# Attention on one core: value products one per step in two of every three steps, in place of one or two in every third step

## The chip, the core and the metric

The kernel runs on one core of a Trainium2 chip. The metric is the device time of one execution in microseconds, the median of several executions. The engines of the core are TensorE (PE, with its weight loads shown apart as PEld), VectorE (DVE), ScalarE (ACT), GpSimd (POOL) and SyncE (SP), which issues most DMAs.

## The reference

One transformer layer over a sequence of 4096 rows of 256 features: attention with 16 heads of 16 features, a residual and a layer norm, then a feed-forward product with int8 weights, a residual and a layer norm. The attention, which is nearly all of the time, is

```python
attn = jnp.einsum('bhqd,bhkd->bhqk', query, key) / scale     # 16 heads, 4096 x 4096 each
attn = jax.nn.softmax(attn, axis=-1)
out = jnp.einsum('bhqk,bhkd->bhqd', attn, value)
out = out.transpose(0, 2, 1, 3).reshape(b, s, d_model)
return out @ Wo_w + Wo_b
```

with query and key each a sum of a plain and a rotary projection. The kernel computes the softmax without a row maximum of its own: a bound on each row's scores is a further row of the stacked query, and the row sum comes from a column of ones beside the values.

## The kernel before, in words

A first stage projects x into keys, queries and values. The attention stage then works on 32 "heads" t: 16 heads times two halves of 2048 queries. A head has 32 key tiles kt of 128 keys, and 4 query blocks j of 512 queries, so 128 blocks of 128x512 scores. The tiles in BY_VECTOR (15, 30 and 31; for t = 0 tile 15 alone) have their exponential computed by VectorE as a polynomial. All other blocks go through ScalarE in groups of two (GROUPS): 62 groups for head 0, 58 for each other head, 1860 groups in all. A group is one step s of the schedule.

For each step TensorE does, in this order (the loop at L613): it waits for ScalarE's exponential of step s (`pe.wait_ge(a.exp, s + 1)`); it computes the two score blocks of step s + 3 (`scores`, L555: K of 49 rows, fp16, one block in each half of the array's rows, side by side); if BLOCK_STEP names the step, it computes one score block for VectorE (`block`); if PROJECT_STEP names it, it projects a finished tile of the first half (`project_first`, L637; 16 such steps, in heads 17 to 22); and it computes the value products that VALUES[s] lists (`values`, L598). A value product is one key tile with all four query blocks: four fp32 matmuls of 128x32 by 128x512 on the four column quarters of the array, which the profile lists as eight records. Scores go to three pairs of PSUM banks in turn (SLOTS = 3), so the scores of step s + 3 may be written only when ScalarE is done with step s.

ScalarE does one ACTIVATE (L797) per step: exp over two banks (128x1024) into a ring of 30 blocks, 15 steps, in SBUF. It waits for the scores of its step, and, where `ring_need` says so, for the value product that frees its place in the ring.

VectorE takes its own blocks out of PSUM one by one (`block_bits`, L833). After four blocks, a cycle, it splits bits (L841, L843), and in the next cycle, behind each block's bits, it does one step of the polynomial of the cycle before (L853, L857). The last of these tells TensorE (b_exp) that the tile may be used for a value product. At a head's end it copies the head's sums out (L807) and norms them (L812 to L826). TensorE computes block n only when the bits of block n - 1 are taken out; it computes the first value product of a head only when the bits of the last block before it are out, and the first block after that only when the copy is done, for these two use the same two banks, 6 and 7, in exchange.

The order is fixed when the program is built. `value_steps` gives the 32 steps of a head's value products: `HEAD_STEP[t] + LAG + k * length // KT`, moved on to the next step with s % 3 == 0. As 32 products fall on some 20 such steps, most of these have two. `make_values` then fills the steps with tiles, each tile no earlier than the step of its last exponential, and tiles of VectorE VECTOR_LATE steps behind the block whose polynomial step finishes them. `make_block_steps` spreads the 12 blocks of a head evenly between TURN[t] + BEHIND and TURN[t + 1] - BEFORE, where TURN[t] is the step of the head's first value product, and moves a block that would fall on s % 3 == 0 on by one.

Of the kernel before, what the change touches and what calls it, by code (L numbers as in the profile page):

```python
# [32 lines left out]
SLOTS, SLOT = 3, 2  # L33
# [22 lines left out]
CYCLES = len(TILES)  # L56
PLACE = {(t, kt, j): (g * SLOT + k) % RING for g, (t, blocks) in enumerate(GROUPS) for k, (kt, j) in enumerate(blocks)}

LAG = 6
VALUE_PHASE = 0  # L60
FIRST_BLOCKS = 14
BEFORE = 4
BEHIND = 5
VECTOR_LATE = 4
URGENT = 6


def value_steps(t):

    length = HEAD_STEP[t + 1] - HEAD_STEP[t]  # L70
    steps = []
    for k in range(KT):
        s = HEAD_STEP[t] + LAG + k * length // KT
        s += (VALUE_PHASE - s) % SLOTS
        steps.append(min(s, STEPS_ALL))
    return steps


VALUE_STEPS = [value_steps(t) for t in range(NT)]
TURN = [steps[0] for steps in VALUE_STEPS] + [STEPS_ALL]  # L80


def make_block_steps():

    steps = []
    for t in range(NT):
        first = TURN[t] + BEHIND if t else 0
        last = TURN[t + 1] - BEFORE if t + 1 < NT else STEPS_ALL - 20
        n = FIRST_BLOCKS if t == 0 else len(BY_VECTOR) * QB
        n = min(n, QB * CYCLES - len(steps))  # L90
        for k in range(n):
            s = first + (last - first) * k // (n - 1)
            s += s % SLOTS == VALUE_PHASE and k < n - 1
            steps.append(s)
    return steps


BLOCK_STEP = make_block_steps()
assert BLOCK_STEP == sorted(BLOCK_STEP) and len(BLOCK_STEP) == QB * CYCLES
COPY_AFTER = {FIRST_BLOCKS - 1 + len(BY_VECTOR) * QB * t: t for t in range(NT - 1)}  # L100
# [12 lines left out]
def make_values():  # L113

    at = [[] for _ in range(STEPS_ALL + 1)]
    for t in range(NT):
# [6 lines left out]
        for s in VALUE_STEPS[t]:  # L123
            urgent = scalar and scalar[0][1] + RING // SLOT - 1 < s + URGENT
            if vector and not urgent and (vector[0][0] <= s or not scalar):
# [1597 lines left out]
```

## Time and profile before

| | before |
|---|---|
| median of 3 runs | 1998.19 us (1994.56 to 1999.97) |
| the profiled execution: its time | 1997.78 us |
| its span, first to last instruction | 1995.9 us |
| attention stage: first exponential starts, last ends | 157.26 and 1899.72 us |
| ACT busy | 1827.3 us, 92% |
| PE busy | 1806.7 us, 91% |
| DVE busy | 1578.7 us, 79% |
| mean granted TensorE clock | 0.981 of full speed |

Busy times are unions of an engine's instructions. Successive instructions of ScalarE overlap in the profile by some 0.1 us, and matmuls by more, so that an engine can be shown busy without a break and still be held up a little at each instruction. Starts of instructions tell more than busy shares.

### The profile page before, as it was taken

How to read it: one execution, taken by the hardware profiler on the slowest of the kernel's cores; microseconds unless marked ns; L12 is line 12 of the kernel's file. 1: busy time of each engine (PE TensorE's matmuls, PEld its weight loads, DVE VectorE, ACT ScalarE, POOL GpSimd, SP SyncE). 2: the span in 40 equal slices, each digit the busy share in tenths (PEclk: the TensorE clock that was granted, in tenths of full speed). 3: DMA queues.
4: the chain of work that ended last, by engine and by line, in shares of the span. 5: the costliest groups of instructions: out<-in, count | busy, mean ns of one | idle time of the engine just before them, and what ended most of it. 6: DMA issues, size and time to landing. Idle time of an engine off the chain costs nothing.

```text
span 1995.9 us, 31796 instructions
## 1 busy us (share of the span) xinstructions
PE 1806.7 (91%) x13009; PEld 490.0 (25%) x13009; DVE 1578.7 (79%) x1500; ACT 1827.3 (92%) x2026; POOL 167.3 (8%) x134
## 2 busy tenths in 40 slices
PE   8967999999999999999999999999999999999965
PEld 3431222222222222222222222222222222222234
DVE  3654887988887888888788888788988988888548
ACT  4448999999999999999999999999999999999925
POOL 5723500000000000000000000000000300000012
PEclk9998999999999999999999999999999999999977
DMA  4654111110111111111121000111111100110012
GB/s 163 215 170 163 25 25 25 25 25 18 21 22 19 21 25 25 24 25 25 25 67 25 19 18 17 22 25 25 25 25 25 25 21 21 21 21 17 1 44 85
DMA packets 165484, 81.48 MB, mean 41 GB/s; under 512 B 130205, under 2 KB 146717, under 8 KB 164857
## 3 DMA queue, kind: packets, MB, share of 16 engines
q1 hardware_dynamic: 164024, 78.11, 15.0%
q8 instruction: 103, 1.69, 0.3%
q10 hardware_dynamic: 1312, 1.32, 0.2%
q14 instruction: 45, 0.36, 0.1%
HBM read 48.83 MB, written 29.23 MB: 39 GB/s over the span
## 4 chain that ended last, share of the span: by engine, by line
ACT 66%; PE 13%; issue 10%; DVE 4%; POOL 2%; DMA 2%; SPq 1%; ACTq 0%; DVEq 0%; POOLq 0%
ACT arena L797 53%; ACT parts_or_sums L797 13%; PE PS L598 7%; PE PS L555 4%; PE PS L637 2%; PE PS L1041 1%; POOL arena L1360 1%; DVE arena L857 1%; DVE bn L725 1%; DMA arena<-arena 1%; DMA Qst<-parts_or_sums 1%; POOL arena L1359 1%; POOL arena L1362 1%; DVE arena L1651 1%; DMA arena<-head_out 0%
## 5 line engine op out<-in xcount | busy, mean ns | idle before, releaser
L797 ACT ACTIVATE arena<-PS 128x1024 f32<-128x1024 f32 x1488 | 1395.0, 1038 | 30.5 <-PE PS L555 29.1
L598 PE MATMUL PS<-arena,Vh 128*32 128x512 f32 x6704 | 1001.2, 600 | 0.8 <-DVE arena L857 0.4
L555 PE MATMUL PS<-Qst,Kst 49*128 49x512 f16 x4096 | 691.3, 384 | 126.8 <-ACT arena L797 77.1
L857 DVE SCALAR_TENSOR_TENSOR arena<-arena 128x2048 f32<-128x2048 f32 x282 | 646.5, 2292 | 0.1
L833 DVE TENSOR_SCALAR arena<-PS 128x512 int32<-128x512 f32 x376 | 259.3, 690 | 286.1 <-PE PS L555 278.1
L555 PEld LDWEIGHTS PS<-Qst,Kst 49*128 49x128 f16 x4096 | 178.5, 93 | 945.5 <-ACT arena L797 710.8
L598 PE MATMUL PS<-parts_or_sums,Vh 128*32 128x512 f32 x1488 | 366.1, 600 | 0.0
L797 ACT ACTIVATE parts_or_sums<-PS 128x1024 f32<-128x1024 f32 x372 | 360.9, 1037 | 3.8 <-PE PS L555 3.4
L598 PEld LDWEIGHTS PS<-arena,Vh 128*32 128x32 f32 x6704 | 195.0, 109 | 340.5 <-issue 331.1
L853 DVE SCALAR_TENSOR_TENSOR arena<-arena 128x2048 f32<-128x2048 f32 x94 | 216.0, 2298 | 0.0
L841 DVE TENSOR_SCALAR arena<-arena 128x2048 int32<-128x2048 int32 x94 | 115.7, 1231 | 7.3
L843 DVE TENSOR_SCALAR arena<-arena 128x2048 int32<-128x2048 int32 x94 | 115.8, 1232 | 0.0
L1380 POOL TENSOR_SCALAR nmr<-mv 128x16 f32<-128x16 f32 x1 | 0.3, 264 | 1231.6 <-DVE mv L1529 1231.6
L1041 PE MATMUL PS<-arena,w 128*128 128x512 f32 x192 | 87.8, 606 | 8.8 <-DMA bias<-biases_dram 6.7
L598 PEld LDWEIGHTS PS<-parts_or_sums,Vh 128*32 128x32 f32 x1488 | 66.0, 109 | 74.4 <-issue 74.4
L1244 ACT ACTIVATE arena<-PS,bias 128x512 f32<-128x512 f32 x56 | 38.1, 687 | 42.8 <-PE PS L1041 33.1
L1041 PEld LDWEIGHTS PS<-arena,w 128*128 128x128 f32 x192 | 37.2, 195 | 56.0 <-issue 55.0
L1464 DVE TENSOR_TENSOR arena<-arena 128x512 f32<-128x512 f32 x16 | 17.3, 1086 | 40.0 <-POOL arena L1362 40.0
L767 POOL TENSOR_TENSOR arena<-arena,rows 128x256 f32<-128x256 f32 x32 | 45.0, 1449 | 39.8 <-DMA arena<-x_dram 39.8
L771 POOL TENSOR_TENSOR arena<-arena,rows 128x256 f32<-128x256 f32 x16 | 11.1, 727 | 342.5 <-ACT arena L757 342.5
L807 DVE COPY parts_or_sums<-PS 128x512 f32<-128x512 f32 x32 | 22.0, 686 | 13.5 <-PE PS L598 13.5
L741 ACT ACTIVATE rstd<-mv,small 128x6 f32<-128x6 f32 (+3 forms) x6 | 1.8, 300 | 32.2 <-DVE mv L729 32.2
(115 smaller groups left out, 615.4 us busy)
## 6 DMA issues: line engine op xcount, KB each, us to landing
Kst<-k_halves SPq DMA_DIRECT2D x64, 128.0 KB
Qst<-q_halves SPq DMA_DIRECT2D x64, 128.0 KB
Vh<-head_values SPq DMA_DIRECT2D x30, 256.0 KB, 4.4
arena<-xT_dram SPq DMA_DIRECT2D x8, 512.0 KB, 5.1
k_halves<-parts_or_sums SPq DMA_DIRECT2D x16, 256.0 KB, 2.4
k_whole<-arena SPq DMA_DIRECT2D x8, 512.0 KB, 3.3
q_halves<-parts_or_sums SPq DMA_DIRECT2D x16, 256.0 KB, 3.2
q_whole<-arena SPq DMA_DIRECT2D x8, 512.0 KB, 4.4
```

What stands on the lines that cost most here:

```text
L555: return nc.tensor.matmul(out, Kst[par][low:low + HK + 1, at:at + 128], Qst[par][low:low + HK + 1, j * CH:(j + 1) * CH], start=True, stop= ...
L598: last = nc.tensor.matmul(bank(value_bank(t))[32 * j:32 * j + 32, :], Vh[t % 2][:, kt, :], moving, start=kt == first, stop=kt == last_kt)
L637: last = nc.tensor.matmul(out, heads_out(t // TH, c, t % TH * 128, 128), w[:, W_O + c * D:W_O + (c + 1) * D], start=c == 0 and starts, sto ...
L767: nc.gpsimd.tensor_tensor(Y[:, t, :], Y[:, t, :], bo, ALU.add).then_inc(s, 1)
L797: nc.scalar.activation(ring(at, k), bank(g % SLOTS * SLOT, k), ACT.Exp, scale=EXP_SCALE).then_inc(a.exp, 1)
L833: nc.vector.tensor_scalar(bits[:, j * CH:(j + 1) * CH].bitcast(int32), bank(block_bank(n)), LOWEST, TO_BITS, ALU.max, ALU.mult).then_inc(b ...
L841: nc.vector.tensor_scalar(mantissa.bitcast(int32), bits.bitcast(int32), 0x007FFFFF, 0x3F800000, ALU.bitwise_and, ALU.bitwise_or).then_inc( ...
L843: nc.vector.tensor_scalar(power.bitcast(int32), bits.bitcast(int32), 0x7F800000, 0x40000000, ALU.bitwise_and, ALU.bitwise_xor).then_inc(b_ ...
L853: nc.vector.scalar_tensor_tensor(out=t, in0=mantissa, scalar=POLY[3], in1=mantissa, op0=ALU.add, op1=ALU.mult).then_inc(b_poly, 1)
L857: last = nc.vector.scalar_tensor_tensor(out=t, in0=t, scalar=POLY[3 - j], in1=power if j == 3 else mantissa, op0=ALU.add, op1=ALU.mult)
L1041: last = nc.tensor.matmul(bank(out_bank), l, r, start=k == 0, stop=k == len(lhsT) - 1)
L1244: nc.scalar.activation(dst[e], bank(e), ACT.Identity, bias=bs[e], scale=scales[e]).then_inc(s_ev, 1)
```

## The change

The value products may now stand on steps with s % 3 of 0 or 1, at most one per step; blocks for VectorE on steps with s % 3 of 2 or 1; and five distances of the plan are shorter. Nothing else is changed: each engine does the same instructions on the same data.

```diff
-LAG = 6
-VALUE_PHASE = 0
+LAG = 4
+VALUE_PHASES = (0, 1)
+BLOCK_PHASES = (2, 1)
 FIRST_BLOCKS = 14
-BEFORE = 4
-BEHIND = 5
+BEFORE = 3
+BEHIND = 4
 VECTOR_LATE = 4
-URGENT = 6
+URGENT = 4
 def value_steps(t):
...
         s = HEAD_STEP[t] + LAG + k * length // KT
-        s += (VALUE_PHASE - s) % SLOTS
+        s = max(s, steps[-1] + 1 if steps else 0)
+        while s % SLOTS not in VALUE_PHASES:
+            s += 1
         steps.append(min(s, STEPS_ALL))
 def make_block_steps():
...
             s = first + (last - first) * k // (n - 1)
-            s += s % SLOTS == VALUE_PHASE and k < n - 1
+            s += s % SLOTS not in BLOCK_PHASES and k < n - 1
             steps.append(s)
```

## Rows read from the trace of the kernel before

**Rows 1.** The page's first part: busy us, share of the span, instructions.
```profile
PE 1806.7 (91%) x13009; PEld 490.0 (25%) x13009; DVE 1578.7 (79%) x1500; ACT 1827.3 (92%) x2026; POOL 167.3 (8%) x134
```
**Rows 2.** Busy time of L797 alone in stretches: us, ACT busy (xcount), clock, DMA.
```profile
157.26:300.00 142.74, 141.74 (x154) 0.96 0.19 53
...
600.00:900.00 300.00, 299.05 (x324) 1.00 0.11 23
...
1090.00:1390.00 300.00, 286.78 (x309) 1.00 0.11 22
...
1600.00:1899.72 299.72, 298.76 (x323) 1.00 0.08 17
sum 1742.46, ACT 1724.04; mean ACT 246.29
```
**Rows 3.** Timeline of ACT around 1075 us: start, us, instruction, count.
```profile
1074.84 2.87 ACT L797 ACTIVATE parts_or_sums<-PS 128x1024 f32<-128x1024 f32 x3
1077.55 11.26 ACT L797 ACTIVATE arena<-PS 128x1024 f32<-128x1024 f32 x12
1088.70 2.92 ACT L797 ACTIVATE parts_or_sums<-PS 128x1024 f32<-128x1024 f32 x3
1091.51 7.54 ACT L797 ACTIVATE arena<-PS 128x1024 f32<-128x1024 f32 x8
```
**Rows 4.** Timeline from 940.9 us, weight loads of PE that begin each piece.
```profile
941.52 0.33 PEld L555 LDWEIGHTS PS<-Qst,Kst 49*128 49x128 f16 x5 [0.84 <-ACT arena L797]
...
942.48 0.16 PEld L598 LDWEIGHTS PS<-arena,Vh 128*32 128x32 f32 x8 [0.29 <-issue]
...
944.34 0.33 PEld L555 LDWEIGHTS PS<-Qst,Kst 49*128 49x128 f16 x5 [0.84 <-ACT arena L797]
...
945.30 0.11 PEld L598 LDWEIGHTS PS<-arena,Vh 128*32 128x32 f32 x1 [0.35 <-issue]
...
946.30 0.10 PEld L555 LDWEIGHTS PS<-Qst,Kst 49*128 49x128 f16 x2 [0.84 <-ACT arena L797]
```
**Rows 5.** Timeline from 1115 us, a step with a projection and those behind it.
```profile
1115.04 0.10 PEld L555 LDWEIGHTS PS<-Qst,Kst 49*128 49x128 f16 x2 [0.84 <-ACT arena L797]
...
1115.36 0.73 PEld L637 LDWEIGHTS PS<-w,ctkv 128*128 128x128 f32 x4 [0.23 <-issue]
...
1116.42 0.10 PEld L555 LDWEIGHTS PS<-Qst,Kst 49*128 49x128 f16 x2 [0.33 <-issue]
...
1116.86 1.02 ACT L797 ACTIVATE arena<-PS 128x1024 f32<-128x1024 f32 x1 [0.36 <-PE PS L555]
...
1117.54 0.16 PEld L598 LDWEIGHTS PS<-arena,Vh 128*32 128x32 f32 x8 [0.42 <-issue]
...
1117.78 1.02 ACT L797 ACTIVATE parts_or_sums<-PS 128x1024 f32<-128x1024 f32 x1
...
1118.54 0.11 PEld L555 LDWEIGHTS PS<-Qst,Kst 49*128 49x128 f16 x4 [0.84 <-ACT arena L797]
1118.85 0.10 PEld L555 LDWEIGHTS PS<-Qst,Kst 49*128 49x128 f16 x2 [0.20 <-ACT parts_or_sums L797]
1119.03 1.94 ACT L797 ACTIVATE parts_or_sums<-PS 128x1024 f32<-128x1024 f32 x2 [0.24 <-PE PS L555]
```
**Rows 6.** Stretch 600 to 900 us: us, busy of PE, PEld, DVE, ACT, POOL.
```profile
600.00:900.00 300.00, 279.83 (x2142) 66.25 (x2136) 248.99 (x208) 299.05 (x324) 0.00 (x0) 1.00 0.11 23
```
**Rows 7.** The page's groups of VectorE's polynomial and bits: busy, mean ns | idle before.
```profile
L857 DVE SCALAR_TENSOR_TENSOR arena<-arena 128x2048 f32<-128x2048 f32 x282 | 646.5, 2292 | 0.1
L833 DVE TENSOR_SCALAR arena<-PS 128x512 int32<-128x512 f32 x376 | 259.3, 690 | 286.1 <-PE PS L555 278.1
```
**Rows 8.** Line L857, who waited for it: us, times.
```profile
  PEld PS L598: 7.8, 20
```
**Rows 9.** The chain that ended last, 1888 to 1908 us.
```profile
1888.29 1.23 DVE arena L843
1889.54 2.30 DVE arena L853
1891.87 2.30 DVE arena L857
1894.19 2.30 DVE arena L857
1896.52 2.30 DVE arena L857
1899.23 8.05 DMA arena<-head_out
1907.99 2.00 PE PS L637 x4
```

## The prediction

> **What bounds the kernel now.** I read the page's busy shares first. ACT is busy 92% and PE 91% of the span [rows 1], which doesn't tell which of them holds the other. Then I looked at the exponentials alone. The attention stage holds 1860 of them between 157.26 and 1899.72 us, 1742.5 us, and in it ACT has hardly a gap: 299.05 of 300 us [rows 2]. That looks like an engine at its limit. The starts say otherwise. Three exponentials that nothing holds up start within 1077.55 - 1074.84 = 2.71 us, 0.904 us each; a little later three take 1091.51 - 1088.70 = 2.81 us [rows 3]. At 0.904 us each the 1860 would need 1859 x 0.904 + 1.03 = 1682 us. So **60.8 us** of the stage is lost in small waits, and the 0.13 us by which instructions overlap in the profile hides most of it.
>
> Where do they come from? In rows 4 and 5 the reader can see TensorE's order, piece by piece:
> - Scores begin 0.05 us after the end of the exponential that frees their banks: an end at 1117.78 + 1.02 = 1118.80, the load at 1118.85 [rows 5].
> - Scores with something else behind them take 0.32 us (1115.04 to 1115.36) [rows 5]; scores followed by scores 0.23 us (five loads of 0.09 us within 0.33 us, so the fifth starts some 0.23 us after the first) [rows 4]. A block for VectorE is one more matmul of the same kind, 0.22 us.
> - Two value products take 944.34 - 942.48 = 1.86 us until the next scores; one takes 946.30 - 945.30 = 1.00 us [rows 4], and again 1118.54 - 1117.54 = 1.00 [rows 5]. So a product is 0.86 us, and each return from values to scores costs 0.14 us once.
> - From the start of late scores to their exponential it is 0.44 us (1116.42 to 1116.86) to 0.49 us (1118.54 to 1119.03) [rows 5].
>
> Put together, with times from the end of exponential s, s a step with two values: scores at 0.05, values at 0.37, the scores of step s + 4 at 2.23, exponential s + 4 at 2.67 to 2.72. ACT alone would start it at 4 x 0.904 - 1.03 = 2.59. It is late by 0.08 to 0.13 us. The plan of before (worked out from the functions shown) has 402 steps with two values: 402 x 0.10 = 40 us, with the slip of the next exponential somewhat more. The rest is elsewhere: from 1090 to 1390 us there are 309 exponentials where other stretches of 300 us have 324 [rows 2], 15 x 0.904 = 14 us for the 16 projections. Some 1 to 2 us are at the stage's start.
>
> **The change part by part.** I write "lag" for how long after the end of exponential s the scores of step s + 3 begin. ACT is not held up as long as the lag is at most 3 x 0.904 - 1.03 - 0.44 = 1.24 us (1.19 with 0.49).
>
> *Removed: the pairs.* Worked out from the new plan, 1022 steps have one value and none within the attention has two. After one value the next lag is 0.05 + 0.32 + 1.00 - 0.904 = 0.47 us. The 0.10 us at 402 places, about 46 us with what follows them, go.
>
> *Added: switches.* Steps with values rise from 619 to 1023, so there are 404 more returns at 0.14 us and as many more turns from scores to values at 0.32 - 0.23 = 0.09 us: 93 us more of TensorE. This lies in TensorE's slack, if it has it. Per three steps TensorE needs, before, 0.32 + 1.86 + 0.23 + 0.23 = 2.64 us with two values and 1.78 us with one. With 402 of 620 triples of the first kind and 376 x 0.22 us of blocks it averages 2.47 us of the 2.71. Afterwards a triple with two values takes 0.32 + 1.00 + 0.32 + 1.00 + 0.23 = 2.87 us, more than ACT's 2.71; the average is 2.62 us, 96.6%. So TensorE still keeps up on average, but nearly two thirds of the triples run behind and the triples with one value catch up.
>
> The Trainium skill says in "TensorEngine Tiling (Array Packing)", section Key Properties, that changing the tiling mode, and not just the tile, drains TensorE; scores (two row halves) and values (four column quarters) are two such modes. The page gives no price; the trace agrees with 1.00 us against 0.86. By the rule this change is made the wrong way round: it buys an even order with drains.
>
> How far does it fall behind? A value step adds 0.32 + 1.00 - 0.904 = 0.42 us to the lag, a step without one takes 0.67 off, a block adds 0.22. The new plan has nearly always two triples with two values, then one with one value. From a lag of 0.05 the six steps give 0.05, 0.47, 0.88, 0.21, 0.63, 1.04: below 1.24. But of the 185 such double runs 172 have one block ahead of that last point: 1.26, late by 0.02 to 0.07 us. That is 3 to 12 us; I take 8. It is a sum of nine pieces, each good to 0.02 us: 0.1 us more would be 17 us more, while 0.1 less gains only those 8. After the triple with one value the lag is 0.05 again, so nothing piles up.
>
> *The projections* keep their 16 steps and 1.06 us each (1115.36 to 1116.42) [rows 5]. Ten of them now stand on s % 3 == 2, behind two value steps: lag about 0.9 to 1.1, then + 0.23 + 1.06 + 0.09 - 0.904, and the next value steps push it on by 0.42 each: 0.8 us or so late each time, against 14/16 = 0.87 before. 13 us stay.
>
> *VectorE.* Its work per head is 248.99 us of 300 [rows 6], 45 us in a head of 58 steps (54.2 us); in a head of 53 us that is 85%. Its blocks have 51 steps in place of 49, so in time they are as far apart as before, 4.2 us, for 3.0 us of bits and polynomial and 2.5 us of split each fourth time. The polynomial that releases a value takes 0.05 + 0.23 + 0.44 + 0.69 + 2.29 = 3.7 us from the exponential ahead of its block [rows 7]; the value is asked for 4 steps later at 3.62 + 0.37 = 3.99 us. This 4-step case, 11 tiles before, is 30 tiles now. TensorE waited for these 20 times, 7.8 us [rows 8]. What is queued behind such a wait are scores, which have some 0.8 us of lag to give, so little of it reaches ACT. At a head's turn the last block stands 3 steps ahead of the value that needs its bank, 2.7 us, for 1.2 us if VectorE is free, 3.5 us if it has just begun a polynomial step. Together I take 4 us, between nothing and 10.
>
> *LAG, URGENT, ring.* In the plan a ring place is asked for at the earliest 3 steps behind its value before, 6 afterwards: no new wait. The DMAs hang on the same counts of scores and on norms that come no later. The start keeps 1 to 2 us, as the first values run at half clock or near it (0.96 on average in the first stretch) [rows 2]. At the end the chain goes from the last block, step 1840 in both plans, over VectorE's polynomial and the load of the heads to the projection [rows 9]; what the last 20 steps gain (0.7 us) is therefore not on the path, and the two values fewer behind the last exponential aren't either.
>
> *The sum.* Lost before 60.8; lost after 8 + 13 + 4 + 2 = 27, and as the errors of the lag reach further up than down I take 33. Gain 60.8 - 33 - 0.7 = 27 us. The profiled execution took 1997.8 us, 0.4 under the median of 1998.2; the forecast is **1971 us**.
>
> The Trainium skill ("Trainium Kernel Development and Optimization", Best Practices) warns against reading matmul busy time as closeness to the limit. Here PE is shown busy 279.8 of 300 us [rows 6], 93%, and 93 us more would give 98%, which sounds like less room than the 96.6% of the sum above.
>
> **Rivals.**
> 1. *All waits but the projections' go.* If each piece is 0.01 us shorter, no run of triples is late: 15 us left, gain 45, **1953 us**. For it: the lateness is 0.02 to 0.07 only. Against: the 0.49.
> 2. *The switch is dearer in this order* (the other side). If the return costs 0.18 and not 0.14 us, four returns add 0.16 us to each of 172 double runs: 27 us, the whole gain, **1998 us**. That is the point from which it decides; at 0.20 it is some 14 us slower, **2012 us**. Against it stand two returns behind single values of 1.00 us in different surroundings [rows 4, 5]; for it, that no row shows value, scores, value without a pause.
> 3. *VectorE becomes the one that is late.* If it runs 1 us behind at the 62 tiles that are wanted 4 or 5 steps after their block, TensorE stands 0.8 us each time with a lag of 0.6 already there, and ACT loses about 0.3: 19 us, **1990 us**. For it: 17% idle become 15%. Against: in the trace it waits for blocks 278 us in all [rows 7].
>
> **How the numbers follow.** The forecast has 0.58 (its own range 1961 to 1982: lost after 22 to 43), rival 1 0.14, rival 2 0.16 (half of it slower, the rest from 1985 to 2003), rival 3 0.12. What can be told from no change is 0.3%, 6 us. Faster by more: 0.58 + 0.14 + 0.07 + 0.05 = 0.84; within: 0.08; slower: 0.08. The range takes in rival 1, the upper bounds of the unknown costs and most of rival 3: 1952 to 1990.
>
> **What would show it.** In 600 to 900 us there should be 327 to 331 exponentials in place of 324, with three starting in 2.71 to 2.75 us everywhere; the stretch of the projections should still be 13 to 15 exponentials short. A single value should still take 1.00 us up to the next scores. Value steps followed by late exponentials should be those of a second triple with two values and a block. L857 should show waits of TensorE of 5 to 15 us. The forecast is wrong if the return costs more than 0.16 us, if exponentials on s % 3 == 2 are late in every triple, or if waits for VectorE exceed 20 us.

## The result and the profile after

The kernel after takes **1986.2 us** (median of 4 runs, 1983.7 to 1987.6) against 1997.7 us before (median of 4 runs too; the 1998.2 of the table above is of 3): ratio 0.994, 95% interval 0.9924 to 0.9956. That is 11.5 us less, where 27 were forecast. The forecast had the direction right and the size wrong, and 1986.2 us lies in its range of 1952 to 1990.

The page's busy shares, which answer to [rows 1]:
```profile
PE 1851.2 (93%) x13009; PEld 451.9 (23%) x13009; DVE 1582.6 (80%) x1500; ACT 1815.3 (92%) x2026; POOL 163.4 (8%) x134
```
The busy time of the exponentials alone (L800 is the old L797), which answers to [rows 2]:
```profile
600.00:900.00 300.00, 300.00 (x328) 1.00 0.12 23
...
1090.00:1390.00 300.00, 287.20 (x310) 1.00 0.10 21
...
sum 1732.20, ACT 1712.21; mean ACT 244.60
```
The quiet stretch has 328 exponentials in place of 324, within the forecast's 327 to 331, and the stretch of the projections is 18 short of that, where 13 to 15 were forecast. The stage took 1732.2 us in place of 1742.5: 10.3 us less. The profiled execution was 14.1 us faster than the one of before; the other 3.8 us lie outside the stage, behind it. There the clock came back sooner: in the 25 us behind the last exponential the granted clock was 0.86 on average, 0.73 before. Both executions begin the projections of the tail at 1.2 GHz (granted clock 0.52 from 1907 to 1920 us before). Before, four tiles took 2.07 or 2.08 us and one 1.76, after, one took 2.07 and one 1.75:
```profile
1897.42 2.07 PE L640 MATMUL PS<-w,arena 128*128 128x256 f32 x4
...
1899.96 1.75 PE L640 MATMUL PS<-w,arena 128*128 128x256 f32 x4
...
1901.95 1.13 PE L640 MATMUL PS<-w,arena 128*128 128x256 f32 x4
```
Whether this belongs to the change is not shown: the stretch behind the last exponential takes 96.2 us in the profiles of before and thin_before, 92.1 and 91.8 in those of after and thin_after (the thin kernels come below), and 93.0 to 95.2 in all others of this study. Between the medians lie 11.5 us, and the profiled stages account for 10.3 of them.

TensorE's pieces, which answer to [rows 4]. The timeline, weight loads that begin a piece:
```profile
441.19 0.10 PEld L558 LDWEIGHTS PS<-Qst,Kst 49*128 49x128 f16 x2 [0.84 <-ACT arena L800]
...
441.52 0.12 PEld L601 LDWEIGHTS PS<-arena,Vh 128*32 128x32 f32 x3 [0.23 <-issue]
...
442.51 0.33 PEld L558 LDWEIGHTS PS<-Qst,Kst 49*128 49x128 f16 x5 [0.84 <-ACT arena L800]
...
443.26 0.11 PEld L601 LDWEIGHTS PS<-parts_or_sums,Vh 128*32 128x32 f32 x2 [0.42 <-issue]
```
Scores 0.33 us, one value 442.51 - 441.52 = 0.99 us, as forecast; over the stage's 1020 single values the median from the first load to the next scores' load is 0.996 us, as it is for the 216 before. The switch costs what it did before.

So where are the missing 15 us? The first surprise is in ScalarE's own rows. The timeline of ACT in the kernel after:
```profile
656.14 3.01 ACT L800 ACTIVATE parts_or_sums<-PS 128x1024 f32<-128x1024 f32 x3
658.99 11.16 ACT L800 ACTIVATE arena<-PS 128x1024 f32<-128x1024 f32 x12
669.89 3.02 ACT L800 ACTIVATE parts_or_sums<-PS 128x1024 f32<-128x1024 f32 x3
```
Three exponentials without a wait took 2.87 us before [rows 3]; here they take 3.01 and 3.02. The same instruction lasts 1.13 us on average in place of 1.04 (the page of after has mean 1134 and 1137 ns for L800, that of before 1038 and 1037 for L797). Nothing in it was changed.

### The profile page after: what moved, and what is told of

The parts are those of the page before. It is cut to its first block, busy times and chain, and to the rows that moved or that the text cites. A ratio compares the mean times of both kernels' runs of the same rounds, so it can differ in the third digit from the quotient of the medians.

```text
span 1981.9 us, 31796 instructions
## 1 busy us (share of the span) xinstructions
PE 1851.2 (93%) x13009; PEld 451.9 (23%) x13009; DVE 1582.6 (80%) x1500; ACT 1815.3 (92%) x2026; POOL 163.4 (8%) x134
## 4 chain that ended last, share of the span: by engine, by line
ACT 69%; PE 10%; issue 9%; DVE 6%; DMA 2%; POOL 2%; SPq 1%; ACTq 0%; DVEq 0%; POOLq 0%
ACT arena L800 55%; ACT parts_or_sums L800 14%; PE PS L601 5%; PE PS L558 3%; PE PS L640 1%; DVE arena L860 1%; PE PS L1044 1%; POOL arena L1363 1%; DVE bn L728 1%; DMA Qst<-parts_or_sums 1%; DMA arena<-arena 1%; POOL arena L1362 1%; DVE arena L1654 1%; POOL arena L1365 0%; DMA arena<-head_out 0%
## 5 line engine op out<-in xcount | busy, mean ns | idle before, releaser
L800 ACT ACTIVATE arena<-PS 128x1024 f32<-128x1024 f32 x1488 | 1396.5, 1134 | 31.4 <-PE PS L558 31.0
L601 PE MATMUL PS<-arena,Vh 128*32 128x512 f32 x6704 | 1082.6, 606 | 5.5 <-DVE arena L860 3.6
L558 PE MATMUL PS<-Qst,Kst 49*128 49x512 f16 x4096 | 710.7, 384 | 61.4 <-ACT arena L800 38.2
L860 DVE SCALAR_TENSOR_TENSOR arena<-arena 128x2048 f32<-128x2048 f32 x282 | 646.4, 2292 | 0.1
L601 PE MATMUL PS<-parts_or_sums,Vh 128*32 128x512 f32 x1488 | 386.0, 604 | 0.0
L800 ACT ACTIVATE parts_or_sums<-PS 128x1024 f32<-128x1024 f32 x372 | 369.3, 1137 | 2.8 <-PE PS L558 2.8
L601 PEld LDWEIGHTS PS<-arena,Vh 128*32 128x32 f32 x6704 | 155.9, 108 | 278.6 <-issue 270.0
L601 PEld LDWEIGHTS PS<-parts_or_sums,Vh 128*32 128x32 f32 x1488 | 53.1, 108 | 59.1 <-issue 59.1
L1362 POOL TENSOR_TENSOR arena<-arena 32x512 f32<-32x512 f32 x16 | 24.4, 1527 | 40.2 <-DMA arena<-arena 40.1
```

The source lines that it names most:

```text
L558: return nc.tensor.matmul(out, Kst[par][low:low + HK + 1, at:at + 128], Qst[par][low:low + HK + 1, j * CH:(j + 1) * CH], start=True, stop= ...
L601: last = nc.tensor.matmul(bank(value_bank(t))[32 * j:32 * j + 32, :], Vh[t % 2][:, kt, :], moving, start=kt == first, stop=kt == last_kt)
L800: nc.scalar.activation(ring(at, k), bank(g % SLOTS * SLOT, k), ACT.Exp, scale=EXP_SCALE).then_inc(a.exp, 1)
L860: last = nc.vector.scalar_tensor_tensor(out=t, in0=t, scalar=POLY[3 - j], in1=power if j == 3 else mantissa, op0=ALU.add, op1=ALU.mult)
L1362: nc.gpsimd.tensor_tensor(b, b, tab[par][:, 1, :], ALU.mult).then_inc(s_rope, 1)
```

## The experiments

"Lost by ends" below is what the stage lost, that is, how much longer it took than its 1860 exponentials alone would, if an exponential takes 0.9167 us from end to end. For the whole stage it is the stage less 1.03 less 1859 x 0.9167 = 1704.1 us; for parts it is summed over the end times of the exponentials' records. The first experiment shows where 0.9167 comes from.

**half_after and half_before: how fast is ScalarE alone?** Half the columns of every value product, in both kernels. As the sums are then incomplete, a second edit, not shown here, holds at zero the flag that starts the kernel's exact second attention. The edit in values:

```diff
-                    moving = poly[c % 2][:, j * CH:(j + 1) * CH] if vector else ring(at)
-                    last = nc.tensor.matmul(bank(value_bank(t))[32 * j:32 * j + 32, :],
+                    moving = (poly[c % 2][:, j * CH:(j + 1) * CH] if vector else ring(at))[:, 0:CH // 2]
+                    last = nc.tensor.matmul(bank(value_bank(t))[32 * j:32 * j + 32, 0:CH // 2],
```

> The kernel after, with each value product cut to half its columns (256 of 512), and the flag that starts the exact second attention held at zero; so the attention sums are incomplete. TensorE has some 0.7 us less to do per three steps and nothing in the stage waits for it, the projections' steps excepted. Theory A (ScalarE's own rate is what the ends of its exponentials show, 0.917 us each, and the 0.904 us between starts is only a start running ahead of the end before): 1860 exponentials take 1706 us and a few more, 1707 to 1716 us from first start to last end, 327 in a quiet stretch of 300 us. Theory B (0.904 us is the rate, as the prediction took it): 1682 to 1692 us, 332 in 300 us.

> The kernel before with the same two edits (half the columns of each value product, flag held at zero). Both theories: the pair of values takes 1.0 us less, so no exponential is late behind it; the order of the value products makes no difference and the stage is within 4 us of the same edit in the kernel after. Theory A: 1707 to 1718 us. Theory B: 1682 to 1694 us.

Measured: 2010.2 and 2018.3 us, one execution each, stages of 1758.2 and 1763.0 us. Both theories missed the time, because less work made TensorE slower: its granted clock fell again and again (last section). Of the 53.0 us that half_after lost by ends 49.1 fall on the 398 distances from end to end that overlap a stretch with the lower clock or the 0.5 us behind it, and of the 57.8 us of half_before 56.2 on 416 of them. Outside these stretches half_before, with its pairs, loses 1.6 us and half_after 3.9: with shorter value products and the clock up, neither order holds ScalarE up by much, as both theories had it. For the pace the long stretches without a wait decide. Timeline of ACT in half_after, the pieces of three at the ring's end:
```profile
284.59 2.94 ACT L800 ACTIVATE parts_or_sums<-PS 128x1024 f32<-128x1024 f32 x3
...
298.16 3.12 ACT L800 ACTIVATE parts_or_sums<-PS 128x1024 f32<-128x1024 f32 x3
...
311.72 3.31 ACT L800 ACTIVATE parts_or_sums<-PS 128x1024 f32<-128x1024 f32 x3
...
325.28 3.50 ACT L800 ACTIVATE parts_or_sums<-PS 128x1024 f32<-128x1024 f32 x3
...
338.84 3.69 ACT L800 ACTIVATE parts_or_sums<-PS 128x1024 f32<-128x1024 f32 x3
```
Starts are 13.56 us apart for 15 exponentials, 0.904 us each. But each piece is 0.19 us longer than the one before, so ends are 13.75 us apart, **0.917 us** each. The start runs ahead of the work by 0.0125 us per exponential until a wait sets it back; here 81 exponentials in a row have no wait, and the last record is 2.0 us long. The median from end to end is 0.917 us in every kernel of this study, the one before included. TensorE waits for ends: in half_after 1160 of the 1857 loads that open a step's scores start 0.050 to 0.060 us behind the end of an exponential, however long its record is. So 0.904 us is the pace of starts, and 0.917 us is the pace of the engine. Of the two theories on the pace A holds, and B has fallen.

At this pace the stage needs 1859 x 0.9167 + 1.03 = 1705.1 us at least. Before it lost **37.3 us**, not 60.8; after it lost **27.0**.

**phases_only and distances_only: which half of the change?** phases_only is the kernel after with the old distances. They are four, LAG, BEFORE, BEHIND and URGENT, and not five, as the section on the change and the expectation of phases_only say:

```diff
-LAG = 4
+LAG = 6
-BEFORE = 3
-BEHIND = 4
+BEFORE = 4
+BEHIND = 5
-URGENT = 4
+URGENT = 6
```

distances_only is the kernel before with the same four lines changed the other way.

> The new steps for value products and blocks, with the five distances as before (LAG 6, BEFORE 4, BEHIND 5, URGENT 6). Theory A with the phases as the cause: the pairs' waits go here too, ratio to before 0.993 to 0.997, lost time of the stage by ends 26 to 31 us against 36.7 before. Rival (the shorter distances bring the gain): ratio 0.999 to 1.002.

> The old steps (values on every third, one or two) with the new distances (LAG 4, BEFORE 3, BEHIND 4, URGENT 4). If the phases are the cause: no gain, and as a tile of VectorE is now wanted sooner and the pairs stay, 2 to 15 us slower than before, with more waits for line L857. If the distances are the cause: ratio 0.993 to 0.997.

Measured: phases_only 1986.1 us, ratio 0.9941 (0.9922 to 0.996), 26.1 us lost by ends. distances_only 2009.0 us, ratio 1.0058 (1.0038 to 1.0077), 51.7 us lost. The whole gain comes with the new steps for values and blocks (these two were not tried apart); in sum the shorter distances add nothing to it and by themselves they cost 11.5 us. By the plan distances_only asks for 50 of VectorE's tiles 4 steps behind their block, the kernel before for 11. What this costs is seen in the wait for VectorE's polynomial, which answers to [rows 8]; the line's view in distances_only:
```profile
  PEld PS L598: 21.3, 50
  PE PS L598: 6.7, 6
```
28.0 us of waits in 56 places against 8.2 in 21 before (the 7.8 in 20 of [rows 8] and one of 0.4 us on the line below it in the view). In the same view of phases_only, whose plan has one such tile, this wait occurs once for each of the two, 0.9 us together; in after, with 30 such tiles, 13 times, 11.6 us.

That after and phases_only lose the same, 27.0 and 26.1 us, is two differences that cancel. After loses 6.6 us at two places in which VectorE is late (steps 256 to 263 and 1520 to 1543, next experiment), phases_only 0.6. And phases_only loses more in the regular run: in steps 120 to 1000 and 1310 to 1840 without steps 252 to 264 and 1512 to 1545 it has 40 exponentials more than 0.05 us late, 6.8 us, and after 24, 2.2 us.

**late6: what of the rest is VectorE's?** VECTOR_LATE 6 in place of 4 in the kernel after.

> The kernel after with VECTOR_LATE 6 in place of 4: a tile of VectorE is asked for at the earliest 6 steps behind the block whose polynomial step finishes it. Theory (two places where VectorE has extra work, the feed-forward weights at its block 50 and the row maxima, make TensorE wait, and TensorE's other waits for L860 are hidden in its slack): the two losses around steps 256 to 263 and 1520 to 1543, 3.8 and 2.6 us, shrink to under 2 us together, the wait of 2.6 us at step 252 goes, 1981 to 1985 us. Rival (waits for VectorE are behind more of what is lost): under 1978 us.

Measured: 1984.3 us, ratio to before 0.9941 (0.9924 to 0.9957), 24.1 us lost against 27.0. TensorE's waits for L860 fell from 11.6 us to 0.7. The loss at steps 256 to 263 went from 3.8 to 0.9; the one around step 1520 stayed (3.2 against 2.8). So the forecast of under 2 us for both together holds for the first place and not for the second. The ratio to before is that of the kernel after, so the times show no gain; the profiles' stages differ by 2.9 us. What delays VectorE at the first place is in the timeline of the kernel after: six pieces of the feed-forward weights, all behind one block.
```profile
388.90 0.68 DVE L1519 TENSOR_TENSOR w<-w,rows 128x512 f32<-128x512 int32 x1
...
392.00 0.43 DVE L1522 CAST w<-w 128x512 bf16<-128x512 f32 x1
392.34 0.68 DVE L836 TENSOR_SCALAR arena<-PS 128x512 int32<-128x512 f32 x1
392.94 2.28 DVE L860 SCALAR_TENSOR_TENSOR arena<-arena 128x2048 f32<-128x2048 f32 x1
...
395.28 0.16 PEld L601 LDWEIGHTS PS<-arena,Vh 128*32 128x32 f32 x8 [3.08 <-DVE arena L860]
```
They push the block's bits and the polynomial step back by 3.5 us, and the value product behind it waits with everything in TensorE's queue. Not all of the 3.8 us is this wait. Behind it TensorE's granted clock fell; the windows view of after:
```profile
396.00:399.40 3.40, 3.40 (x19) 0.63 (x15) 3.37 (x4) 2.23 (x3) 0.00 (x0) 0.50 0.00 0
```
thin_after (below) has the same order at this place and the same wait, 3.07 us, but no fall of the clock, and loses 2.2 us there. So some 1.6 us of the 3.8 are the clock's.

The second place has another wait, which VECTOR_LATE does not touch. The timeline of after:
```profile
1571.98 2.27 DVE L765 TENSOR_REDUCE absmax<-arena 128x1 f32<-128x2048 f32 x1
1574.18 0.68 DVE L836 TENSOR_SCALAR arena<-PS 128x512 int32<-128x512 f32 x1
...
1574.92 0.19 PEld L601 LDWEIGHTS PS<-arena,Vh 128*32 128x32 f32 x8 [2.23 <-issue]
```
By the plan step 1516 has the first value product of a head, and step 1513 the last block before it, whose bits must be out first (the wait for b_bits in `values`). The row maximum (L765) stands ahead of these bits, and the value product starts 0.06 us behind their end. In late6 the same wait is 2.22 us, and the clock fell behind it, 1.8 us lost in steps 1514 to 1523 becoming 3.3; the smaller loss of after in steps 1534 to 1543, 1.1 us behind a wait for L860, is gone.

**any_step: pile-up or switches?** The kernel after with

```diff
-VALUE_PHASES = (0, 1)
-BLOCK_PHASES = (2, 1)
+VALUE_PHASES = (0, 1, 2)
+BLOCK_PHASES = (0, 1, 2)
```

> The kernel after with value products and blocks allowed on every step (VALUE_PHASES and BLOCK_PHASES 0, 1, 2), still at most one product per step: mostly every second step has one, with two in a row about once in ten steps. The same work and the same number of switches as after. Theory (what is lost outside VectorE's places is TensorE's lag piling up over consecutive value steps, at the projections above all): lag never passes 0.9 us without a projection, and a projection's loss falls from 1.0 to some 0.4 us each; stage 1717 to 1724 us against 1732.2, total 1973 to 1979 us. Rival (the switches between scores and values are the cost): no gain over after, 1984 to 1988 us.

Measured: **1976.4 us**, ratio to before 0.9899 (0.9882 to 0.9915), stage 1723.0 us, 17.8 us lost. The number of steps with values, and so of switches, is the same 1023, so the switches alone are not what is lost; where they stand counts. 6.5 of the 9.2 us gained against the kernel after are at the projections: 9.8 us lost in steps 1000 to 1310 against 16.3, 0.6 us per projection in place of 1.0, where 0.4 was expected. The windows of the exponentials in any_step:
```profile
600.00:900.00 300.00, 300.00 (x329) 1.00 0.12 23
1090.00:1390.00 300.00, 292.42 (x319) 1.00 0.10 21
```
319 in the stretch of the projections against 310, and 329 against 328 elsewhere.

**thin_after and thin_before: what a projection costs.** The 16 projections inside the attention cut to 32 of 256 columns:

```diff
-                project_tile(n, bank(project_bank(n))[:, 0:D]).then_inc(p_proj, 1)
+                for k in range(2):
+                    last = nc.tensor.matmul(bank(project_bank(n))[:, 0:32], heads_out(0, k, n * 128, 128),
+                                            w[:, W_O + k * D:W_O + k * D + 32], start=k == 0, stop=k == 1)
+                last.then_inc(p_proj, 1)
```

> The kernel after with the 16 projections inside the attention cut to 32 of their 256 columns, so the first half's tiles are incomplete. By ends the steps 1000 to 1310 lose 16.2 us after. If the projections' 1.06 us each are the cause, 1 to 4 us are left; if it is VectorE's extra work there (statistics and norms, adding tiles), 10 us or more are left.

> The kernel before with the same cut of the projections. By ends the steps 1000 to 1310 lose 17.9 us before. With the pairs still there, 4 to 6 us are left (3.8 us is what 310 ordinary steps lose), so the pairs' whole price over the stage is some 20 us and not 40 or 47.

Measured: 8.8 us left in steps 1000 to 1310 in the order after (of 16.3), 11.0 in the order before (of 18.0). Both lie above what was expected. The edit was weaker than I took it to be (and it is one execution of each kernel); in thin_after, timeline:
```profile
1105.19 0.52 PEld L612 LDWEIGHTS PS<-w,ctkv 128*128 128x128 f32 x4 [0.23 <-issue]
...
1105.75 0.11 PEld L601 LDWEIGHTS PS<-parts_or_sums,Vh 128*32 128x32 f32 x2
```
A projection still takes 1105.75 - 1105.19 = 0.56 us of the 1.06 [rows 5], nearly all of it weight loads. So 16 x 0.50 = 8.0 us less work gave back 7.5 and 7.0 us: what a projection takes beyond TensorE's slack is lost almost one for one, in either order. What the remaining 8.8 us are made of, between the other half of the projections, TensorE's short average slack and VectorE's additions, was not taken apart. Outside these steps thin_before loses what before does (11.0 and 6.3 us in steps 120 to 1000 and 1310 to 1840, in both).

**best and best_lag6: together.** any_step with VECTOR_LATE 6 and VectorE's extra work spread:

```diff
-            hooks.update({NORM_BLOCK + n: lambda n=n: first_norms(n) for n in range(TH)})
-            hooks.update({NORM_BLOCK + TH + 4 * q: lambda q=q: first_largest(q) for q in range(2)})
-            hooks.update({40: check_range, 50: ffn_weights})
+            hooks.update({NORM_BLOCK + 2 * n: lambda n=n: first_norms(n) for n in range(TH)})
+            hooks.update({NORM_BLOCK + 2 * TH + 4 * q: lambda q=q: first_largest(q) for q in range(2)})
+            hooks.update({40: check_range})
+            hooks.update({50 + 2 * m: lambda m=m: ffn_weights(m) for m in range(6)})
```

(`ffn_weights(m)` is the m-th of its six instructions.)

> Values and blocks on any step, VECTOR_LATE 6, and VectorE's extra work spread: the six steps of the feed-forward weights behind every second block from block 50 on in place of all behind block 50, the 16 norms and two row maxima behind every second block. any_step loses 17.8 us by ends: 3.1 around step 256, 1.9 at 1532, 2.2 in the first steps, 9.8 at the projections. The first two should go: 12 to 14 us lost, stage 1718 to 1720 us, total 1971 to 1975 us. If these losses come from the step at which the tile is asked for and not from the extra work, no gain over any_step, 1976 us.

> The same with LAG 6: the first value product comes two steps later, so the stage's first 20 steps, in which TensorE runs at half clock, should lose 1.1 us as before and not 2.2. Otherwise as the kernel with LAG 4: 1970 to 1974 us. If the earlier values were what gave the gain of the new order, it would be lost here: 1980 us or more.

Measured: **1973.2 us**, ratio 0.9878 (0.9862 to 0.9895), and 1972.5 us, ratio 0.9875 (0.9858 to 0.9893); the two can't be told apart. The intervals of best and any_step overlap too, so what best gains over any_step rests on the profiled stages, 1717.1 and 1723.0 us. best loses 11.9 us by ends: 9.8 at the projections, 1.7 in the first 20 steps, 0.4 in all the rest. The losses of 3.4 and 2.4 us in steps 120 to 1000 and 1310 to 1840 of any_step are gone (which of the three edits took which was not tried). Moving the first values two steps later changes nothing (1.6 us in the first 20 steps): that expectation missed. The timeline of ACT in best, beside the three rows of after above:
```profile
652.72 3.24 ACT L800 ACTIVATE parts_or_sums<-PS 128x1024 f32<-128x1024 f32 x3
655.43 11.53 ACT L800 ACTIVATE arena<-PS 128x1024 f32<-128x1024 f32 x12
666.33 3.38 ACT L800 ACTIVATE parts_or_sums<-PS 128x1024 f32<-128x1024 f32 x3
```
The less ScalarE waits, the longer its records: 2.7 us and more for starts of three, 3.24 to 3.38 for the work.

## Why the prediction was wrong, step by step

What the stage lost by ends, in us, by steps:

| steps | before | after | phases_only | any_step | best |
|---|---|---|---|---|---|
| 1 to 120 | 1.9 | 2.0 | 0.9 | 2.2 | 1.7 |
| 120 to 1000 | 11.0 | 5.2 | 5.1 | 3.4 | 0.0 |
| 1000 to 1310, projections | 18.0 | 16.3 | 17.0 | 9.8 | 9.8 |
| 1310 to 1860 | 6.4 | 3.5 | 3.1 | 2.4 | 0.5 |
| whole stage | 37.3 | 27.0 | 26.1 | 17.8 | 11.9 |

- **"Lost 60.8 us": the step that failed.** It took 0.904 us, the distance of starts, for ScalarE's pace. With 0.917 us the loss before is 37.3; the other 1859 x (0.9167 - 0.904) = 23.6 us could not be gained by any order. A row could have hinted at it: a record of 1.02 us [rows 5] and two more starts 0.904 us apart end after 2.83 us, and the row shows 2.87 [rows 3], so the ends moved apart faster than the starts. half_after settled it.
- **The pairs.** That exponentials behind two values are late was right, and they are not late any more. The price, 46 us, was taken against the wrong pace. Steps 120 to 1000 and 1310 to 1840, three quarters of the stage, lost only 17.3 us before from all causes, which is 17.3 x 1860 / 1410 = 23 us for the whole stage. This term was sized at twice what there is. The trace of before puts all of it on the pairs: in these steps 139 exponentials are more than 0.05 us late, and each is exponential s + 4 of a step s with two values, the place that the prediction worked out; the 307 pairs there cost 0.058 us each, not 0.10. The same sum with the right pace gives it: ScalarE alone would start exponential s + 4 at 4 x 0.917 - 1.03 = 2.64, so 2.67 to 2.72 is late by 0.03 to 0.08 us.
- **Lost after: 27 us by the sum,** 27.0 measured by ends. I then took 33. That the sum fits is in part luck, for the single terms are off both ways. Double runs with a block were given 8 us, and outside the projections and VectorE's two places about 2 us are lost (steps 120 to 1000: 5.2, of which 3.8 at 256 to 263; steps 1310 to 1840: 3.5, of which 2.8 at 1520 to 1543). The wrong pace is behind this term too: with 0.917 the lag at the point in question is 1.20 us and not 1.26, and the limit 1.28 (1.23 with 0.49) and not 1.24, so no such run need be late. The place was right: the 24 exponentials that are more than 0.05 us late all stand behind a second triple with two values and a block. The projections were given 13, they are the greater part of 16.3. VectorE was given 4, its two places cost 6.6, some 1.6 of it by the clock.
- **The switches.** 0.996 us for a single value, as taken; TensorE had the slack for 404 more. Rival 2 did not happen, and any_step shows that as many switches go with 9.2 us less loss. A return from values to scores costs 0.14 us (a second value in a row adds 1.854 - 0.996 = 0.858 us, one by itself takes 0.996), and TensorE's slack hides it. The drain that the Trainium skill names in "TensorEngine Tiling (Array Packing)", Key Properties, agrees with this price; no run here shows that the 0.14 us is the drain.
- **VectorE.** That a 4-step distance is tight was right. The head's turn with the last block 3 steps ahead was named too, and is the second of the two places. What the prediction left out is that both need extra work of VectorE (the feed-forward weights, a row maximum) to cost anything, and that TensorE's clock can fall behind such a wait. Rival 3's mechanism exists (28.0 us of waits in distances_only, 11.6 in after), but in the kernel after little of it reaches ScalarE outside the two places.
- **Rival 1** came nearest in its mechanism (the regular run of steps loses 2.2 us and no more), with 17 us of projections and the wrong pace instead of its 45 us of gain.
- **What stayed** (ring, start, end of the chain) was right: the first 20 steps lose 1.8 us, and the chain ends over the last block and the heads' load again.

With the loss before put right and the other terms left as they were, the forecast is 37.3 - 27 - 0.7 = 9.6 us, or 1988.6 us; measured 1986.2. The closeness owes something to the luck in the 27.

## What to carry to other kernels

To find an engine's own pace, take the distance of ends over a stretch, and look whether the records of equal instructions grow: growing records meant here that starts ran ahead of the work, and the distance of starts flattered the engine. When an experiment thins out an engine's work, compare the granted clock of each stretch first: here it fell, and a second effect came in with the edit. When, as in this kernel, an in-order engine feeds another with two steps of room, spread its work as evenly as the steps allow, even at the cost of more switches, as long as its average load has room; the gain is bounded by what the fed engine really loses. Single pieces of extra work on a third engine (weights, norms, projections) are then what is left, and they want to be spread too.

## What the runs showed of the hardware

- **Less work made TensorE slower.** With half the columns of each value product the kernel took 2010.2 us against 1986.2 (one execution), and the order of before 2018.3 against 1997.7. Windows of half_after (PE, PEld, DVE, ACT, POOL, then clock):
```profile
630.00:660.00 30.00, 25.35 (x215) 5.92 (x207) 23.99 (x18) 29.23 (x33) 0.00 (x0) 0.91 0.05 16
660.00:690.00 30.00, 25.83 (x205) 6.21 (x205) 23.86 (x22) 28.81 (x33) 0.00 (x0) 0.83 0.14 25
690.00:720.00 30.00, 24.01 (x221) 6.33 (x225) 26.80 (x25) 30.00 (x35) 0.00 (x0) 1.00 0.09 29
```
The granted clock falls again and again to its lower level of 1.2 GHz for a while, as in 660 to 690 us with a mean of 0.83, and there single exponentials come up to 1.1 us late, three of them 1.6 to 2.6 us. In the same three windows of the kernels before and after it is 1.00. In the profiles with full value products the clock stands at 2.4 GHz from some 10 us behind the stage's start to its end, but for one or two short stretches in after, late6, any_step and distances_only. So in this stage the full value products also keep the clock up.
- **One wait can cost the clock, and need not.** In after TensorE's weight loads stood 3.08 us, up to 395.28 us, for VectorE's polynomial, and from 396.0 to 399.4 us the granted clock was 0.50. In thin_after it stood 3.07 us at the same place, and the clock stayed at 1.00.
- **ScalarE's records overlap, and no bound was seen here:** 1.02 us long behind a wait, 2.0 us after 81 exponentials without one, at a pace of 0.917 us.
